# Attention with a mixture of experts on one core: four rounds of scattering rows instead of three, and every round written out

## The reference, cut to what matters

```python
xn = layernorm(x)                                  # x: 16 x 512 x 256
qg, kv = split_heads(xn @ Wqg), split_heads(xn @ Wkv)      # 16 heads, keys 16, values 64
q, k, v = l2norm(qg[..., :16]), l2norm(kv[..., :16]), l2norm(kv[..., 16:])
attn = square(relu(q @ k.T))
out = tanh_norm(attn @ v) * tanh(silu(qg[..., 16:]))
attention = merge_heads(out) @ Wout
scores = sigmoid(xn @ router.T)                    # 16 experts in 4 groups, 2 groups, 4 experts a token
moe = sum over the token's 4 experts of w * (silu(xn @ gate_e.T) * (xn @ up_e.T)) @ down_e.T
      + the same of one shared expert of width 256
return x + attention + moe
```

## Time and profile before

| | |
|---|---|
| median of 3 runs | 3211.16 us (3207.59 to 3214.01) |
| the profiled execution's own time | 3214.0 us |
| its span, first to last instruction | 3212.3 us |
| mean granted clock of TensorE | 0.916 |
| PE, DVE, ACT, POOL busy | 71%, 57%, 48%, 44% |

### The profile page before, as it was taken

How to read it: one execution, slowest core, us unless ns; L and a number is a source line. 1 busy time by engine, 2 the same in 40 slices (tenths; PEclk the granted TensorE clock), 3 DMA queues, 4 the chain that set the end, 5 groups by cost and what they waited for, 6 DMA issues and landing times.

```text
span 3212.3 us, 44962 instructions
## 1 busy us (share of the span) xinstructions
PE 2270.3 (71%) x13476; PEld 1213.0 (38%) x13477; DVE 1835.0 (57%) x2961; ACT 1533.6 (48%) x2396; POOL 1429.4 (44%) x1339
## 2 busy tenths in 40 slices
PE   4324638176377877787878788787777788787887
PEld 3322213032143434343443444344343444344343
DVE  6678417164165656556565656556565655646575
ACT  2314416154155555454454545455455545545565
POOL 1112756647544353544445354444435354444521
PEclk9999869688689999999999999999999999999999
DMA  9992442514323140322213131222313132221300
GB/s 348 323 340 71 157 128 80 170 53 158 115 32 55 24 65 19 59 35 40 47 29 59 17 60 31 47 42 34 51 25 60 24 55 40 38 49 28 60 7 7
DMA packets 161549, 247.60 MB, mean 77 GB/s; under 512 B 14945, under 2 KB 147041, under 8 KB 159361
## 3 DMA queue, kind: packets, MB, share of 16 engines
q1 hardware_dynamic: 99104, 164.63, 16.5%
q0 software_dynamic: 62208, 79.99, 15.2%
HBM read 147.84 MB, written 144.25 MB: 91 GB/s over the span
## 4 chain that ended last, share of the span: by engine, by line
PE 36%; issue 18%; DVE 17%; POOL 12%; DMA 9%; ACT 6%; SPq 0%; DVEq 0%; ACTq 0%; POOLq 0%
PE wk L1180 16%; PE av L1264 8%; POOL slot_d L1105 6%; PE acc L1180 5%; DMA xrow<-xn_d 3%; DMA xt_d<-xhl 2%; DMA slot_d<-xrow,slot_no 2%; POOL out_t L1087 2%; ACT ring L945 2%; DVE v L642 2%; POOL hle L1078 2%; DVE pr L660 2%; PE wk L1272 2%; PE sim L1249 2%; DVE ye L680 2%
## 5 line engine op out<-in xcount | busy, mean ns | idle before, releaser
L660 DVE TENSOR_TENSOR pr<-ring 128x1024 f32<-128x1024 f32 x512 | 626.1, 1225 | 440.3 <-ACT ring L945 439.9
L945 ACT ACTIVATE ring<-sim 128x1024 f32<-128x1024 f32 x512 | 524.0, 1023 | 307.9 <-PE sim L1249 287.9
L1264 PE MATMUL av<-pr,v 128*64 128x512 f32 x2048 | 567.0, 635 | 21.2 <-ACT wide L979 19.2
L1087 POOL DMA_INDIRECT out_t<-ye,xg x288 | 474.0, 1646 | 108.4 <-issue 108.4
L1078 POOL TENSOR_TENSOR hle<-hfe,hhe 128x256 f16<-128x256 f32 x208 | 244.9, 1178 | 491.8 <-ACT hhe L956 491.5
L710 DVE TENSOR_TENSOR gate_sb<-gate_sb,wk 128x512 f32<-128x512 f32 x128 | 87.7, 685 | 402.6 <-PE wk L1339 402.6
L1105 POOL DMA_INDIRECT slot_d<-xrow,slot_no x256 | 282.9, 1105 | 76.3 <-issue 58.5
L1135 POOL TENSOR_TENSOR pr<-wide,pr 128x512 f16<-128x512 f32 x128 | 161.6, 1267 | 266.4 <-ACT pr L991 266.4
L667 DVE SCALAR_TENSOR_TENSOR hfe<-wk,up_scale,sge 128x256 f32<-128x256 f32 x208 | 100.4, 483 | 299.0 <-ACT sge L951 295.9
L1073 POOL TENSOR_TENSOR gate_sb<-ring,gate_sb 128x512 f16<-128x512 f32 x128 | 164.3, 1308 | 239.6 <-ACT gate_sb L931 239.6
L951 ACT ACTIVATE sge<-wk,inv_m 128x256 f32<-128x256 f32 x208 | 99.0, 476 | 357.6 <-PE wk L1180 357.5
(11 more groups left out here) (223 smaller groups left out, 4662.6 us busy)
## 6 DMA issues: line engine op xcount, KB each, us to landing
xg<-slot_d SPq DMA_DIRECT2D x147, 258.0 KB, 2.7
slot_d<-pad_rows SPq DMA_DIRECT2D x8, 4644.0 KB, 19.4
xrow<-xn_d SPq DMA_DIRECT2D x64, 512.0 KB, 4.3
xs<-x SPq DMA_DIRECT2D x16, 512.0 KB, 5.0
xn_d<-xs SPq DMA_DIRECT2D x16, 512.0 KB, 19.6
xt_d<-xhl SPq DMA_DIRECT2D x16, 512.0 KB, 17.4
xhl<-xt_d SPq DMA_DIRECT2D x16, 512.0 KB, 3.4
out_t<-pr POOLq DMA_DIRECT2D x16, 512.0 KB, 6.2
```

The lines of the kernel that those rows point to most:

```text
L660: tt(pr[:, n:n + 2, :], ring[:, q:q + 2, :], ring[:, q:q + 2, :], ALU.mult).then_inc(square_done, 1)
L945: a(ring[:, q:q + 2, :], sim[:, :, :], ACT.Relu).then_inc(relu_done, 1)
L1087: pool.indirect_dma_start(out=out, out_offset=bass.IndirectOffsetOnAxis(xg[:, n % XG, j, D + 1:D + 2].bitcast(U32), 0), in_=ye[:, n % 2, j ...
L1264: ins = mm(av[64 * half:64 * half + 64, :], v32[:, j, h * DV:(h + 1) * DV], pr[:, (2 * s + half) % NH_, :], start=(j == 0), stop=(j == NB ...
```

## The change

Rounds of kind B are now 4 to 15. Rounds 0 to 3 are of kind A, and each scatters 16 tiles: `plan_steps` puts an item `RW` into every second step of kind A, and POOL's `item` sends one tile for it; the other engines have nothing for `RW`. The last round, 15, is of kind B. All 16 rounds are written out, with no loop on any engine, so every count is a constant; SP doesn't load tokens beyond the last round. PE's `value_load` stands in XT, two steps earlier than in GU, ahead of the transposes, and its address is a constant.

```diff
-EXP0, EXP1 = 3, 15
-LOOP0 = EXP0 + 2
+EXP0, EXP1 = 4, 16
-SCATTER_AT = [22, 21, 21]
+SEND = TILES // EXP0
...
+    if kind == "A":
+        for k in range(SEND):
+            steps[STEPS // SEND * k].append(("RW", k))
...
         def loops(eng, body):
-            for b in range(LOOP0):
-                body(Round(b, "A" if b < EXP0 else "B", b % 2))
-            with eng.Fori(LOOP0, EXP1, 2) as b:
-                body(Round(b, "B", LOOP0 % 2))
-                body(Round(b + 1, "B", 1 - LOOP0 % 2))
-            body(Round(EXP1, "A", EXP1 % 2, last=True))
+            for b in range(B):
+                body(Round(b, "B" if EXP0 <= b < EXP1 else "A", b % 2, b == B - 1))
...
-                for _ in range(SCATTER_AT[b]):
+                for _ in range(SEND):
                     sp.wait_ge(rows_sent[tau % 2], 16 * TOP * (tau // 2))
...
                 sp.wait_ge(g_full, b * NP_)
-                load_x(b + 1, 1 - odd)
+                if b + 1 < B:
+                    load_x(b + 1, 1 - odd)
...
-            for b in range(EXP0, LOOP0):
+            for b in range(EXP0, EXP1):
                 body(b, b % 2)
-            with sp.Fori(LOOP0, EXP1, 2) as b:
-                body(b, LOOP0 % 2)
-                body(b + 1, 1 - LOOP0 % 2)
...
                 elif kind == "SC":
                     send_block(r, n)
+                elif kind == "RW":
+                    send_rows()
...
                 item(r, ("HH", 1))
-                if isinstance(r.b, int) and r.b < EXP0:
-                    for _ in range(SCATTER_AT[r.b]):
-                        send_rows()
...
                     elif kind == "XT":
+                        g = (r.b - EXP0) * PR + n
+                        col[n] = pe.value_load(blk_w[0:1, g:g + 1], min_val=0, max_val=(E - 1) * P)
                         turn_block(r, n)
                     elif kind == "GU":
-                        g = (r.b - EXP0) * PR + n
-                        col[n] = pe.value_load(blk_w[0:1, bass.ds(g, 1)], min_val=0, max_val=(E - 1) * P)
                         routed_up(r, n, col[n])
```

More of the change, by code:

```diff
@@ L136, in n @@
             count = self.b * (per + extra) + (c - EXP0 * extra)
-            return max(count, 0) if isinstance(self.b, int) else count
+            return max(count, 0)
         done = 0 if self.b < EXP0 else EXP1 - EXP0
```

## The result

The changed kernel takes 3091.6 us (median of four runs, 3089.7 to 3096.4) against 3212.6 of the kernel before; the ratio is 0.9625, with a 95% interval of 0.9606 to 0.9645. That is 121 us less, where the forecast of 3129 us had 82 less.

The account below looks back on a forecast made before the run. Scatter rounds were taken as POOL-bound, block rounds as PE-bound. From a profiled 3214.0 us, -100.4 + 43.4 - 3.0 - 24 + 11 - 9 = -82 gave 3132, less 2.8 to the median 3129 us; range 3093 to 3160.

Parts of the forecast that it names:

- item 5: Register load moved from GU to XT: 1.9 us a round gained behind DN, 2.7 lost ahead of XT; net +11 us.
- item 6: PE's clock in block rounds: fewer low stretches with denser code, half the difference taken, -9 us; bounds -46 and +9.
- Items 1 and 2: Scatter rounds: 16 tiles instead of 22, 21 and 21 gain 100.4 us; a fourth scatter round loses 43.4.
- Item 3: Last round now has blocks but skips the next QK projections: its tail 42.5 us instead of 45.5, -3.0.
- Item 4: Ten rounds leave the hardware loop: 1.6 us in steps, 0.6 in seam, 0.2 in tail, each round; -24 us.
- the clock stays up: Rival: all block rounds run like round 4, clock term -46 instead of -9, 3092 us; chance 0.14.
- the bad bounds together: Rival: clock stays as in the loop (+9) and load fully exposed behind GU (+38), 3174 us; chance 0.14.
- The rival that would have ended slower: All 144 register loads put their whole 0.84 us on PE's path ahead of XT: 121 us, time 3239; chance 0.03.

Follow-up runs that it names:

- experiment 3: The kernel before with only the scatter spread over four rounds of 16 tiles, blocks in rounds 4 to 15, hardware loop kept for rounds 6 to 13: 3137.6 us, ratio 0.983.
- experiment 4: The changed kernel with the register load put back from XT into GU, its address still a constant: 3093.2 us, ratio 0.9692 to the kernel before.
- experiment 6: The changed kernel with a second register load of the same value in GU, besides the one in XT: 3128.3 us, ratio 0.9785 to the kernel before.
- experiment 5: The changed kernel itself, unaltered, timed again in a later job: 3082.8 us, ratio 0.9638 to the kernel before; once more 3083.0 us, 0.9651.
- experiment 1: The kernel before with all rounds written out, no hardware loop on any engine, and nothing else changed: 3149.3 us, ratio 0.9858.

## Why the prediction was wrong, and where it was right

The forecast was 3129 us, 37 above what was measured. The scatter was priced right; the blocks gave 65 us where the sum had 25, and of these 40 us some 25 are item 5 and some 15 item 6.

**Items 1 and 2, the scatter, were right:** -57.0 forecast, -57.7 in the profile (2.1 of it ahead of round 0), 50 to 52 in the profiles of experiment 3's job. So was what they rest on, that POOL sends its tiles back to back whatever the plan's steps say (16 tiles in 106 us as forecast), and that what stands behind them moves up with their end.

**Item 3 was too large.** The last tail is 44.7 us and not 42.5. The row that it was read from belongs to a round without blocks, and a block round has the last block's work in its tail. -0.8 instead of -3.0.

**Item 4, seams and tails, was right for the seams and lucky for the tails:** with item 3 that is 11 us forecast, 10.6 measured. The seams are 5.3 us shorter, for 6 forecast. The tails are 5.4 shorter, 0.8 of it in the last one, for 5 forecast; but that isn't the 0.2 us a round of register work, it is five tails instead of one at a granted clock of 1.00, which take 44.1 us and not 45.6, less one of 47.1. The prediction took the tail of round 4, 45.5, for the only one, and round 3 of before already had one of 44.1. The Trainium skill's rule on taken branches (Runtime: NRT & Kernel Launch, "Instruction fetch mechanics") would have put the gain in the jumps back. The traces don't put it there: the seams inside a pair of rounds, 29.0 to 29.2 us, fell to 28.6 like those with the jump, 29.1 to 29.3. So what went is spread over all rounds, as the 3709 sequencer instructions that are gone would be; whether it is these was not tried alone.

**Item 5 failed in its sign:** +11 forecast, -13 to -14 measured over the block rounds (experiment 4 against the changed kernel; -16 to -18 in their steps alone), some 25 us of the 40. The gain behind DN was right: six gaps of 0.31 us are gone, 2.0 us a round for 1.9. The loss ahead of XT was put at 6 x 0.45 = 2.7 us a round, and it measured 1.2: in round 7 of the changed kernel four times 0.3 to 0.4 (as at 1564.08) and nothing at the other two (as at 1530.47). The step that failed is "the sequencer is hardly ahead there": three or four of GU's matmuls had yet to start when the load began, and they covered about half of the 0.75 us from the load's start to XT; six or seven covered all of it. A second, smaller step was to put the loads of the other six blocks at nothing: their waits for `xel` became 0.4 to 0.7 us a round shorter. The bounds held this (-23), but the sum took a value between them with no row for it.

**Item 6 was too small:** -9 forecast for the clock. With the load left in GU the steps fall by 38.4 us from 1299.3 to 1260.9, where item 4's 16 and item 6's 9 make 25; so 13 more than forecast. Over the whole block rounds it is 2193.8 to 2142.0, 51.8 us, for 36 of items 3, 4 and 6: 16 more. Both set a profile of one job beside one of another, in which the kernel before was 15 us faster, so the size is less sure than that of item 5. The rival "the clock stays up" had this at 3092, and that is the time that was measured, though by two terms and not by one: its own premise, all rounds like round 4 at 0.98, did not come about (0.963 on average). That its time fits is luck.

**The range** ended at 3093. The text says that it takes in the rival of the clock, but that rival's time is 3092, so the bound itself was 1 us off; items 5 and 6 near their good bounds together were left out of it, while the bad bounds together were weighed as a rival. They are not independent. In experiment 6 a gap on PE's path costs its length and about as much again, by the clock (46.9 us for some 23 of gaps), so there both terms go the same way. Between experiments 4 and 5 they didn't: the clock stayed within 0.006. The rival that would have ended slower, a load fully exposed ahead of XT, is excluded: even with two loads the kernel is 2% faster than before.

**What stays open.** Which single gap brings on a low stretch was not settled; the same kernel has rounds at 0.95 and at 0.98, and in its profile of the first job the steps with one low stretch more have a tail with one less behind them. The parts of the 13 us of item 6 that are the clock and code (experiment 1 has 105.8 a round, experiment 4 105.1) were not separated either.

## What to carry to other kernels

A queue that works through a block of independent sends ahead of something on the critical path is priced by one row, the wait for what stands behind it; spreading the block over more rounds helps as far as other work covers it, and putting its pieces into the queue's own idle stretches helps more (81.4, 44.2, then 12.5 us of waiting). A plan that names steps paces an engine only if that engine waits for something in these steps. A buffer of two tiles can add a wait for data to each piece of such a block; look for it before the pieces are moved. A register load of PE's sequencer belongs ahead of a wait that PE has anyway (11 and 17 us here) or behind enough queued matmuls; elsewhere count what the matmuls that have yet to start don't cover, and up to twice that, for its length and for the clock. When the clock moves, add steps and tails before you compare rounds.

## What the runs showed of the hardware

The register load takes 0.30 us, and the next matmul starts 0.75 us or more after the load does. How much PE idles depends on the matmuls that have yet to start by then: 0.31 us lost behind six short ones of `down`, 0.24 us or more where three or four of GU's had yet to start, nothing where six or seven had. Six more gaps of 0.3 us a round lowered the mean granted clock of the steps from 0.967 (experiment 5) to 0.952 (experiment 6) and doubled their price; with the gaps moved and not added (experiment 4) the clock was 0.963. The tails of block rounds took 44.1, 45.6 or 47.1 us at a granted clock of 1.00, 0.96 or 0.93. A jump back of the hardware loop showed no more than 0.1 us; the loop's cost was spread over all rounds.
